# Two attention layers on one core: context kept by a copy, values laid in place by DMA, eight heads per score visit, softmax sums carried in the value tile

## The reference

```python
x = x + jnp.tanh(g_xattn[0]) * _L0_xattn_ref(_layernorm(x, axis=-1), ctx_1024, ...)
x = x + jnp.tanh(g_ffn[0]) * _L0_ffn_ref(_layernorm(x, axis=-1), ...)
x = x + jnp.tanh(g_xattn[1]) * _L1_xattn_ref(_layernorm(x, axis=-1), ctx_1024, ctx_1024, ...)
x = x + jnp.tanh(g_ffn[1]) * _L1_ffn_ref(_layernorm(x, axis=-1), ...)
# L0_xattn: 16 heads of 64; L1_xattn: 16 heads of 16; both
#   attn = softmax(q @ k.T * scale); out = (attn @ v) @ Wo
# L0_ffn: 8 experts, gate weights under 0.1 dropped, out += w_e * (x @ expert_w[e] + expert_b[e])
# L1_ffn: a top-2 mixture with swiglu, which changes only the first 512 tokens
```

## Time and profile before

| | us |
|---|---|
| median of 3 runs | 4108.32 (4107.78 to 4108.96) |
| the profiled execution, its own time | 4109.0 |
| its span, first to last instruction | 4107.3 |
| TensorE busy | 3985.3 (97%) |
| VectorE busy | 2786.6 (68%) |
| ScalarE busy | 2242.6 (55%) |
| GpSimd busy | 1061.3 (26%) |
| mean granted TensorE clock | 0.991 of full speed |

### The profile page before, as it was taken

The page is one execution under the profiler, slowest core; times in us unless marked ns, Lnnn a source line. Parts: engine busy times, 40 slices in busy tenths (PEclk is TensorE's granted clock), DMA queues, the critical chain, the costliest instruction groups (busy, mean ns, idle before and its releaser), DMA issues.

```text
span 4107.3 us, 95418 instructions
## 1 busy us (share of the span) xinstructions
PE 3985.3 (97%) x32788; PEld 3282.9 (80%) x32788; DVE 2786.6 (68%) x6496; ACT 2242.6 (55%) x4201; POOL 1061.3 (26%) x1303
## 2 busy tenths in 40 slices
PE   5999999999999999999999999999999999999968
PEld 4788888888888888888888888888888888888845
DVE  4667667666766766766766766666676676676646
ACT  4555555555555565565555555555556556556521
POOL 2222222222322322222222222232232222222210
PEclk9999999999999999999999999999999999999979
DMA  2000000000000000000000000000000000000001
GB/s 84 14 15 9 15 14 9 15 14 12 11 14 12 11 15 14 9 15 14 9 15 14 9 15 14 11 13 14 12 11 14 15 9 15 14 9 15 10 18 61
DMA packets 57907, 64.80 MB, mean 16 GB/s; under 512 B 5232, under 2 KB 54672, under 8 KB 57104
## 3 DMA queue, kind: packets, MB, share of 16 engines
q10 hardware_dynamic: 34688, 32.52, 2.6%
q1 hardware_dynamic: 23184, 31.81, 2.3%
HBM read 47.01 MB, written 17.30 MB: 16 GB/s over the span
## 4 chain that ended last, share of the span: by engine, by line
PE 94%; DVE 3%; issue 1%; ACT 1%; DMA 1%; POOL 0%; DVEq 0%; SPq 0%; POOLq 0%; ACTq 0%
PE g L660 29%; PE g L666 16%; PE scores L660 12%; PE scores L802 11%; PE g L816 6%; PE scores L756 6%; PE scores L785 3%; PE g L723 3%; DVE x_nm L1064 2%; PE g L680 2%; PE scores L760 1%; PE g L734 1%; PE scores L789 1%; PE g L741 1%; PE g L690 1%
## 5 line engine op out<-in xcount | busy, mean ns | idle before, releaser
L581 ACT ACTIVATE prob<-scores 120x1024 f32<-120x1024 f32 x512 | 510.9, 1024 | 382.1 <-PE scores L760 249.6
L1027 DVE TENSOR_TENSOR an<-scores,inv 64x256 f32<-64x256 f32 x1024 | 424.4, 414 | 289.8 <-ACT inv L604 281.9
L459 POOL TENSOR_TENSOR q_lo<-an,q_hi 128x256 fp32r<-128x256 f32 x512 | 371.8, 731 | 753.5 <-ACT q_hi L620 752.6
L1125 DVE SCALAR_TENSOR_TENSOR x<-g,lg_w,x 128x256 f32<-128x256 f32 x1024 | 494.9, 483 | 103.3 <-PE g L660 72.2
L802 PE MATMUL scores<-prob,vx 120*128 120x256 f32 x2048 | 540.6, 386 | 3.6 <-DVE an L1027 2.4
L660 PE MATMUL g<-ew_hi,yT_hi 128*128 128x512 f32 x1024 | 488.6, 477 | 0.6 <-DVE x L1117 0.6
L802 PEld LDWEIGHTS scores<-prob,vx 120*128 120x128 f32 x2048 | 367.0, 189 | 72.5 <-issue 3.7
L1064 DVE TENSOR_REDUCE y_nm<-g 128x4 f32<-128x480 f32 x512 | 301.0, 650 | 173.5 <-PE g L734 173.5
L604 ACT ACTIVATE inv<-inv 64x512 f32<-64x512 f32 x640 | 404.0, 631 | 20.3
L660 PE MATMUL g<-ew_lo,yT_hi 128*128 128x512 f32 x1024 | 405.6, 396 | 0.0
L660 PE MATMUL g<-ew_hi,yT_lo 128*128 128x512 f32 x1024 | 403.0, 394 | 0.0
(11 more groups left out here) (207 smaller groups left out, 9668.9 us busy)
## 6 DMA issues: line engine op xcount, KB each, us to landing
x_in<-in_x ACTq DMA_DIRECT2D x64, 256.0 KB, 2.9
out<-y_x SPq DMA_DIRECT2D x64, 256.0 KB, 2.1
ctx_in<-in_ctx ACTq DMA_DIRECT2D x128, 120.0 KB, 2.4
wk_s<-in_gu SPq DMA_DIRECT2D x8, 512.0 KB, 3.5
wk_s<-in_wq SPq DMA_DIRECT2D x1, 1024.0 KB, 4.8
wv_s<-in_wo SPq DMA_DIRECT2D x1, 1024.0 KB, 4.7
wk_s<-in_ew SPq DMA_DIRECT2D x1, 1024.0 KB, 4.9
wv_s<-in_ew SPq DMA_DIRECT2D x1, 1024.0 KB, 4.9
```

Source lines behind the costliest of these rows:

```text
L459: g.tensor_tensor(q[1][:, p, :], an[:, p % 3, :], q[0][:, p, :].bitcast(F32), ALU.subtract).then_inc(x_attn_lo.sem, 1)
L581: a.activation(prob[:, e % 2].rearrange("p o u s -> p (o u s)"), scores[0:NK, banks, :].rearrange("p o c -> p (o c)"), ACT.Exp, scale=scal ...
L1027: ins = v.tensor_tensor(dst[64 * o:64 * o + 64, :], pvo[0:64, cols], inv[:, k, cols], ALU.mult)
L1125: ins = v.scalar_tensor_tensor(out=x1[:, t, :], in0=ring.bank(Y_FFN[j])[:, o * D:(o + 1) * D], scalar=lg_w[:, t, 2 * n + o:2 * n + o + 1], ...
```

## The change

What it does, in six parts:

- **Context.** `p_load` and `p_ctx` go. `p_hold`, a DMA from ACT's queue, copies `ctxT` into a second tile `ctx_y`, which `y_k` and `y_v` read. The copy of the next context into `ctxT` (L504 in the new text) waits for it.
- **Values of layer 0.** ACT copies `n_v` into a dense tile `v_new`; a new step `n_vx` lays it into `vx` by a DMA of 120 x 8 pieces of 64 numbers (256 bytes). `x_pv` 0 and 4 wait for it.
- **Score visits.** `x_st` has two visits instead of four; each does two groups of four heads, into banks 0 and 1, then 2 and 3.
- **x_pv in the ring.** Since `scores` is full, the eight `x_pv` and `z_out` become ring jobs; `x_out` writes `scores` bank 0.
- **Sums of layer 1.** `vx1` is set to 1.0, and the values fill 16 of a head's 32 columns; the other 16 stay ones. A product now yields values and sums together: each of the two `y_pv` visits has 8 products, where two adjoining visits had 16. DVE then turns the bank in blocks of 32 x 32 (`STREAM_TRANSPOSE`), takes a reciprocal of the sums, multiplies, and turns back: four dependent instructions in place of two. ACT's Ln and Exp for layer 1 go.
- **ORDER** is written anew, so nearly every step has another neighbour and another bank.

```diff
@@ -48,22 +48,21 @@
 ORDER = (
...
-    ("y_pv", 0), ("y_pv", 1), ("y_mul", 0), ("p_wt", 0), ("y_pv", 2), ("y_pv", 3), ("n_v", 1), ("p_eb", 0),
+    ("n_vx", 0), ("n_q", 2), ("n_q", 3), ("p_tr2", 0), ("n_max", 0), ("y_st", 0), ("n_max", 1), ("p_gate", 0),
+    ("n_res", 0), ("p_wt", 0), ("y_pv", 1), ("n_vx", 1), ("n_maxt", 1), ("p_eb", 0), ("y_hi", 0), ("y_mul", 1),
...
-FILLS = ("n_ctx", "n_tr", "n_k", "n_v", "n_q", "n_max", "n_maxt", "p_tr2", "p_gate", "p_lg", "p_ctx", "p_wt", "p_eb",
-         "y_pv", "y_k", "y_v", "y_ffn", "y_tr3", "y_q", "y_max", "y_maxt")
+FILLS = ("n_ctx", "n_tr", "n_k", "n_v", "n_q", "n_max", "n_maxt", "p_tr2", "p_gate", "p_lg", "p_wt", "p_eb",
+         "x_pv", "z_out", "y_pv", "y_k", "y_v", "y_ffn", "y_tr3", "y_q", "y_max", "y_maxt")
...
+        vx, v_new = sb("vx", [P, H, P]), sb("v_new", [NK, 2, H // 2 * DH0])
+        ctx_y = sb("ctx_y", [P, KD, NK])
-        VX1 = H * P + 4 * DH1 + P
-        vx1 = sb("vx1", [P, VX1])
+        vx1 = sb("vx1", [P, H * P])
+        turned, y_an, y_sums = sb("turned", [P, HR1, S // 32, 32]), sb("y_an", [P, S // 32, HR1, DH1]), sb("y_sums", [P, HR1, S // 32])
-        vx1_rows = vx1[:, 0:2 * H * DH1].rearrange("p (j s c) -> p j s c", s=2, c=2 * DH1)
-        ones1 = vx1[:, 2 * H * DH1:2 * H * DH1 + 4 * DH1].rearrange("p (s c) -> p s c", s=2)
+        vx1_rows = vx1[:, 0:2 * H * DH1].rearrange("p (h c) -> p h c", c=2 * DH1)
+        y_turned, y_attn = signal("y_turned", 4), signal("y_attn", 2)
...
                 ring.full(act, i, X_CTX)
+                ctx_held.wait(act, i, 0)
...
+            def hold(i, _):
+                ring.empty(act, i, X_CTX)
+                act.dma_start(ctx_y[:], ctxT[:]).then_inc(ctx_held.sem, 16)
+
+            def x_vx(i, c):
+                ring.empty(act, i, X_V[c])
+                act.dma_start(vx[0:NK, 8 * c:8 * c + 8, 0:DH0],
+                              v_new[:, c, :].rearrange("p (h d) -> p h d", d=DH0)).then_inc(v_moved[c].sem, 16)
 
...
             def x_v(i, c):
+                v_moved[c].wait(act, i, 0)
                 ring.full(act, i, X_V[c])
-                ring.has_emptied(a.copy(vx[0:NK, 8 * c:8 * c + 8, 0:DH0],
-                                      ring.bank(X_V[c])[0:NK, :].rearrange("p (h d) -> p h d", d=DH0)), X_V[c])
+                ring.has_emptied(a.copy(v_new[:, c, :], ring.bank(X_V[c])[0:NK, :]), X_V[c])
...
+                ring.has_emptied(a.copy(vx1_rows[0:NK, :, 0:DH1],
+                                        ring.bank(Y_V)[0:NK, 0:D].rearrange("p (h d) -> p h d", d=DH1)), Y_V)
...
-                x_scored.wait(act, i, g + 1)
-                if g >= 2:
-                    x_mixed.wait(act, i, 2 * g - 2)
-                exp(g, slice(0, 2), SCALE0, x_probs)
+                for e in (2 * g, 2 * g + 1):
+                    x_scored.wait(act, i, e + 1)
+                    if e >= 2:
+                        ring.full(act, i, X_PV[2 * e - 3])
+                    exp(e, slice(e % 2 * 2, e % 2 * 2 + 2), SCALE0, x_probs)
...
-                        y_mixed.wait(act, i, 1)
-                    elif e == 3:
                         ring.full(act, i, Y_PV[0])
...
-                x_mixed.wait(act, i, p + 1)
+                ring.full(act, i, X_PV[p])
                 if p >= 2:
-                    x_attn.wait(act, i, p - 1)
-                invert(pv[p % 2][64:128, :], inv[:, p % 2, :], x_logged, x_recip, i, p + 1)
-
-            def y_pv(i, e):
-                if e % 2 == 1:
-                    m = e // 2
-                    ring.full(act, i, Y_PV[m])
-                    invert(ring.bank(Y_PV[m])[64:128, :], inv[:, m, :], y_logged, y_recip, i, m + 1)
+                    ring.empty(act, i, X_PV[p - 2])
+                invert(ring.bank(X_PV[p])[64:128, :], inv[:, p % 2, :], x_logged, x_recip, i, p + 1)
...
+                at = g % 2 * 2
...
+                for e in (2 * g, 2 * g + 1):
+                    if g >= 1:
+                        x_probs.wait(pe, i, e - 1)
+                    scores_of_quad(e, lambda rows, p: both(kT, rows, p, ALL),
+                                   lambda rows, p: both(q, rows, p, ALL), x_nmT).then_inc(x_scored.sem, 1)
...
             def x_pv(i, p):
                 x_probs.wait(pe, i, p // 2 + 1)
-                if p == 0:
-                    ring.all_empty(pe, i, X_V)
-                if p >= 2:
-                    x_attn.wait(pe, i, p - 1)
-                elif p == 1:
-                    y_made.wait(pe, i - 1, 0)
+                ring.to_fill(pe, i, X_PV[p])
+                if p % 4 == 0:
+                    v_moved[p // 4].wait(pe, i, 16)
                 for o in range(2):
-                    ins = t_.matmul(pv[p % 2][:, o * S:(o + 1) * S], vx[0:NK, 2 * p + o, :], prob[:, p // 2 % 2, o, p % 2, :],
+                    ins = t_.matmul(ring.bank(X_PV[p])[:, o * S:(o + 1) * S], vx[0:NK, 2 * p + o, :], prob[:, p // 2 % 2, o, p % 2, :],
                                     start=True, stop=True)
-                ins.then_inc(x_mixed.sem, 1)
-
-            def y_pv(i, e):
-                job, half = Y_PV[e // 2], e % 2
-                y_probs.wait(pe, i, e + 1)
-                if half == 0:
-                    ring.to_fill(pe, i, job, Y_V)
+                ring.has_filled(ins, X_PV[p])
+
+            def y_pv(i, m):
+                y_probs.wait(pe, i, 2 * m + 2)
+                ring.to_fill(pe, i, Y_PV[m], Y_V)
                 for h in range(HR1):
-                    for row, weights in ((0, lambda o: vx1_rows[0:NK, 2 * e + o, h, :]),
-                                         (64, lambda o: ones1[0:NK, h, :])):
-                        for o in range(2):
-                            at = row + 32 * o
-                            ins = t_.matmul(ring.bank(job)[at:at + 32, half * S:(half + 1) * S], weights(o),
-                                            prob[:, half, o, h, :], start=h == 0, stop=h == HR1 - 1)
-                if half == 0:
-                    ins.then_inc(y_mixed.sem, 1)
-                else:
-                    ring.has_filled(ins, job)
+                    for j in range(ROWS4):
+                        ins = t_.matmul(ring.bank(Y_PV[m])[32 * j:32 * j + 32, h * S:(h + 1) * S],
+                                        vx1_rows[0:NK, HPM * m + HR1 * j + h, :], prob[:, j // 2, j % 2, h, :],
+                                        start=True, stop=True)
+                ring.has_filled(ins, Y_PV[m])
 
...
             def x_out(i, c):
                 t, k0 = c // 2, (c % 2) * 4
-                if c == 0:
-                    x_attn.wait(pe, i, NPAIR)
                 x_attn_lo.wait(pe, i, k0 + 4)
-                ins = products(pv[0][:, t * D:(t + 1) * D],
...
             def y_k(i, _):
-                ring.to_fill(pe, i, Y_K, Y_CTX)
+                ctx_held.wait(pe, i, 16)
...
             def y_out(i, _):
                 y_attn_lo.wait(pe, i, 2)
+                ring.to_fill(pe, i, Y_OUT)
                 for t in range(T):
-                    ins = products(pv[1][:, t * D:(t + 1) * D],
+                    ins = products(ring.bank(Y_OUT)[:, t * D:(t + 1) * D],
                                    [(both(q1, ALL, k, slice(t * P, (t + 1) * P)),
                                      (w1o_s(0)[:, k, :], w1o_s(1)[:, k, :])) for k in range(KD)])
-                ins.then_inc(y_out_in.sem, 1)
+                ring.has_filled(ins, Y_OUT)
...
-                normalised(pv[p % 2], p % 2, an[:, p % 3, :]).then_inc(x_attn.sem, 1)
+                ring.has_emptied(normalised(ring.bank(X_PV[p]), p % 2, an[:, p % 3, :]), X_PV[p])
 
             def y_mul(i, m):
-                y_recip.wait(dve, i, m + 1)
-                ring.has_emptied(normalised(ring.bank(Y_PV[m]), m, an[:, m, :]), Y_PV[m])
+                ring.full(dve, i, Y_PV[m])
+                ring.has_emptied(v.transpose(turned[:].rearrange("p h b c -> p (h b c)"), ring.bank(Y_PV[m])[:]), Y_PV[m])
+                ring.empty(dve, i, Y_PV[m])
+                v.reciprocal(y_sums[:], turned[:, :, :, DH1]).then_inc(y_turned.sem, 1)
+                y_turned.wait(dve, i, 2 * m + 1)
+                v.tensor_tensor(y_an[:].rearrange("p b h d -> p h b d"), turned[:, :, :, 0:DH1],
+                                y_sums[:].unsqueeze(3).broadcast_to([P, HR1, S // 32, DH1]), ALU.mult).then_inc(y_turned.sem, 1)
+                y_turned.wait(dve, i, 2 * m + 2)
+                v.transpose(an[:, m, :], y_an[:].rearrange("p b h d -> p (b h d)")).then_inc(y_attn.sem, 1)
...
```

99 lines of the change are left out of this document (40 added, 59 removed).

## The result

The changed kernel takes **4007.69 us** (median of 4 runs, 4003.99 to 4010.78), the kernel before 4108.42 beside it (4107.78 to 4108.96). The ratio is 0.9755, 95% interval 0.9738 to 0.9771: 101 us less. The forecast was 3972.0, in a range of 3935 to 4050. The direction and the range held; the gain was forecast as 136 us and is 101. The time lies outside the stretch that the prediction held likeliest (3950 to 3995, chance 0.45) and in the one for VectorE late or margins used up (3995 to 4050, 0.24).

A forecast was written before the change was run, and what follows sets the result against it. TensorE's own work was taken to bound the kernel (94% of the chain): 2.46 us a turn spared, less two stalls of 0.15, gives 2.16; over 63 turns 136 us, so 3972 us, range 3935 to 4050.

The forecast's parts named there:

- VectorE late or margins used up: Rival: y_mul of 2.7 us at the turn's end, 4032 us, or thin margins used; 3995 to 4050, chance 0.24.
- Sums: Layer 1 y_pv visits: half the instructions spare 1.73 us, plus probably 0.16 of issue before the second; 1.85 taken.
- (a): End of turn: TensorE stalls for VectorE, whose y_mul 0 precedes the last maxima and wT; 0 to 1.0, 0.15 taken.
- all waits vanish: Rival: the new order also removes TensorE's old stall before n_max 3, 2.81 us a turn, 3931 us; chance 0.17.
- y_mul: VectorE's four-step layer 1 division: 1.8 us each, 1 us more than before; 2.7 if block transposition is slow.
- Context: Second context transposition, 0.21 us a turn on TensorE's chain, is spared.
- Score visits: Two x_st visits fewer, each costing 0.10 to enter and 0.10 to leave: 0.40 us a turn spared.
- Wait (b): Middle of turn: y_ffn 6 waits for x_pv 2's bank, free at F+3.3 against 3.18 of TensorE work; 0.15 taken.
- signs of being wrong: Wrong if TensorE waits at x_pv or expert fills 0.3 or more each turn, transposition exceeds 1 us, or value copy 20.
- margins at zero: Other ring places (x_pv 2, y_max 0, second x_out): thin margins, 0 to 0.3 us put on them, 0 for the sum.
- The ring: Rival, too small: x_pv and z_out share four banks; gain gone at 0.27 us wait each, 4237 at 0.5; slower 0.06.
- The value copy: Layer 0 value DMA of 960 pieces: lands in 2.4 to 19 us, hidden by 24 us, so costs nothing.

The follow-up runs named there:

- before, collision put in: Kernel before, with only GpSimd's residual addition x_res (n_res) moved from ahead of p_stat to behind it: 4109.45 us beside 4109.93, ratio 1.0001.
- before, sums and their order: Kernel before with layer 1 sums; n_v 1 and n_max 3 between y_mul 0 and p_wt, n_max 2 behind p_gate, n_maxt 1 behind second y_pv: 3991.11 us.
- changed, residual later: Changed kernel with one more wait: GpSimd's x_res addition starts only when VectorE has finished p_norm: 3980.77 us, ratio 0.9686.
- and inversion first: Changed kernel, x_res held until p_norm ends, plus ScalarE's inversion of x_pv 2's sums ahead of the fourth exponential: 3979.99 us (inversion edit alone 4006.88).
- and product first: Third edit, on top of the x_res wait and the earlier inversion: VectorE's x_mul 2 ahead of the addition of y_ffn 5: 3950.84 us, ratio 0.9618.
- and division later: Fourth edit, on the three-edit kernel: y_mul split, its reciprocal, product and second transposition moved to a step behind p_wt: 3937.52 us, ratio 0.9588.

## Why the prediction was right, and where its size was off

The median distance between turns, of each kernel:

| kernel | us a turn | time, us |
|---|---|---|
| before | 60.86 | 4108.42 |
| before, collision put in | 60.86 | 4109.45 |
| before, context part | 60.64 | 4097.36 |
| before, sums, old order | 60.8, 26 times 62.2 to 62.7 | 4145.70 |
| before, sums and their order | 58.97 | 3991.11 |
| changed | 59.17 | 4007.69 |
| changed, residual later | 58.73 | 3980.77 |
| and inversion first | 58.73 | 3979.99 |
| and product first | 58.31 | 3950.84 |
| and division later | 58.13 | 3937.52 |

**Sums.** Forecast 1.85 spared and 0.15 given back at (a), 1.70 net. Measured 1.89 net, on the kernel before. The visits came out at 1.00 and 1.05, near the 1.03 worked out from steps of four side by side: 1.68 less. From start to start p_wt takes 0.39 for 0.59, and n_v 1 takes 1.41 where it was 1.63 with p_eb behind it, which began 0.06 after VectorE had wT. This 0.22 is a wait of the old order that the prediction left out. From n_max 1 to y_st 1 it was 3.42 and is, with n_max 3 in its new place, 2.82 + 0.85 = 3.67, the new wait of 0.32 at p_lg among it. So the 0.35 of the rival "all waits vanish" did not come as a gain: in that kernel a wait of about this size stands at p_lg. Wait (a), put at 0.15, cost nothing in the changed kernel and 0.18 once the collision was taken out of it. What the prediction didn't see is how much hangs on the move of n_v 1 and n_max 3 between the two visits. It read "the second visit has now other work before it" as a matter of 0.16; the kernel with the sums alone shows that without it the whole part is a loss.

**y_mul.** Forecast 1.8 us, measured 1.96 from 2063.19 to the next instruction's start at 2065.15:

```profile
2063.19 0.71 DVE L1019 STREAM_TRANSPOSE turned<-g 128x512 f32<-128x512 f32 x1
2063.93 0.25 DVE L1021 RECIPROCAL y_sums<-turned 128x16 f32<-128x16 f32 x1
...
2064.68 0.45 DVE L1026 STREAM_TRANSPOSE an<-y_an 128x256 f32<-128x256 f32 x1
```

0.69 for the block transposition from the reduction of the earlier trace rows was right to 0.02, and the rival with 2.7 us fell.

**Context.** 0.21 forecast, 0.22 measured alone.

**Score visits.** 0.40 forecast. The two visits of the changed kernel take 4.15 us from start to the next step's start where four took 4 x 1.13: 0.37. This was not run alone; but 60.86 - 1.89 - 0.22 - 0.37 = 58.38 is what the three parts should give together, and the kernel with three edits has 58.31. That the two meet to 0.07 is in part chance: the first has the wait of 0.32 at p_lg in it, the second wait (a).

**Wait (b), the term that was mis-sized.** 0.15 forecast, 0.39 on TensorE and 0.42 on the turn. TensorE's side of it was right: from F, the end of x_pv 3, 1.59 + 1.71 = 3.30 (forecast 3.18). The chain on the other side was put at F + 3.3 and took 3.64, from 2025.49 to the product's end at 2029.13. I had taken F as the start of the next step of TensorE. Its products were done only 0.35 later: the visit of eight x_pv instructions starts at 2023.85 and is 1.99 long, so it ends at 2025.84, and the exponential starts at 2025.88. Starts are right for what TensorE does next, and too early for who waits for its result. The step y_ffn 6 is an expert fill that waits by more than 0.3 in every turn, so one of the prediction's own signs of being wrong came true. The forecast also left out the second cause, the addition ahead of the product on VectorE.

**The step that failed: margins at zero.** The prediction walked through the ring and put 0 on its margins, with every duration taken from the kernel before, and the stretch of queries and maxima is not among them. One of these durations doesn't hold in the new order: p_norm, two times 412 ns before, 1.70 us after, since x_res was moved onto it. `n_res` and p_norm were both among the moved steps, and the queue of `n_res` is GpSimd's; it should have been followed there, and set beside what VectorE does in that moment. Worth 0.44 us a turn, by the run with the residual later. The turn without it, 58.73, is the 58.7 that the prediction named, which is in part luck: (b) cost 0.27 more than its term, and the sums brought 0.19 more.

Together: 1.89 + 0.22 + 0.37 - 0.42 - 0.44 = 1.62, against 60.86 - 59.17 = 1.69 measured, and 63 x 1.69 = 106 against the 105.1 by which the span fell. Of the 0.47 a turn that are missing from 2.16, the collision is 0.44 and (b) 0.27 more than forecast, with 0.19 more from the sums on the other side; 0.05 is left unexplained. These terms come from different kernels, so they need not add up exactly.

**The rivals.** "All waits vanish" (3931) was not what the change did. The kernel with four edits comes near it in time (3937.52), but the wait that this rival says goes is still in it. "VectorE late" has the right engine and the wrong place: not y_mul at the end of the turn, but p_norm in the middle. The ring is large enough: no x_pv or expert fill but y_ffn 6 waits in every turn. The value copy landed in 3.6 us, near the lower end of 2.4 to 19, by the DMA issues on the page of the changed kernel (count, KB each, median us from issue to landing):

```profile
vx<-v_new ACTq DMA_DIRECT2D x128, 240.0 KB, 3.6
```

## What to carry to other kernels

A shorter step on the bounding engine uncovers what its length had hidden. Look up what each engine does beside it, and move other work there in the same edit; here that decides between 36 us lost and 117 us gained.

When an edit moves a step on an engine that isn't the bottleneck, set it beside what the other engines do at its new time, and not only behind what it waits for. And if one cause of a wait is removed and nothing moves, look for the instruction at the head of the waiting engine's queue before giving the wait up: there can be two causes of one length.

## What the hardware showed

**GpSimd can hold up VectorE.** In the changed kernel the first p_norm instruction takes 1377 ns and the second 401; in the kernel with the collision put in, 840 and 403 (one line's instructions of each, duration min, median, max):

```profile
L967 DVE TENSOR_SCALAR xn<-x,y_mv,y_rstd x2: 401/889/1377, 2053.1 to 2054.4; 128x256 f32<-128x256 f32 x2
```

```profile
L986 DVE TENSOR_SCALAR xn<-x,y_mv,y_rstd x2: 403/622/840, 2042.4 to 2043.2; 128x256 f32<-128x256 f32 x2
```

The start is 2053.06 and x_res ends at 2054.29, so the long one ends 0.15 after x_res; in the other kernel it is 2042.40 + 0.84 = 2043.24 against 2043.08, 0.16 after. The distance is 0.15 to 0.16 in all 63 turns of both kernels, though p_norm starts 0.06 after x_res in one and 0.6 in the other. So it is not slowed but held until GpSimd is through, and GpSimd's 1.29 us don't change. In both GpSimd starts first; the other order was not looked at. q_lo, with one operand in PSUM, runs beside x_res at its usual length (0.69 at 2041.79). The Trainium skill ("SBUF — State Buffer", Who interferes with whom) has it so: VectorE in its two-port modes, which `tensor_scalar` can enter, and GpSimd share a pair of ports that the first to start keeps for its whole instruction, while the other blocks. Both runs agree, to 0.01 us in the end of the block. No run here shows the mode itself.

**The DMA issue of many pieces is longer in the sequencer.** An issue on ScalarE's queue took 0.36 us and the value copy's takes 0.95. Its bytes are not the reason: the load of x_in in the same queue, 256 KB to the copy's 240, takes 0.40 (L508 at 2067.52 in the changed kernel). Its 960 pieces are the likely one, but no run varies them alone. It cost nothing in this place. Timeline of ScalarE's queue, the kernel with the residual later:

```profile
2039.31 0.95 ACTq L519 DMA_DIRECT2D vx<-v_new  x1
```
